# A four-layer graph kernel: two of the gated layer's turns issued together, a new order for the last groups of the message layer, and a new place for VectorE's first gated slots

## What is computed

```
x = layernorm(x + attention(x))        # exp(8 tanh(QK/8)) * adj, row sums, A @ x @ v
x = layernorm(x + gated(x))            # 5 steps: m = adj h; r, z = sigmoid(..); hv = tanh(..); h = (1-z) h + z hv
x = layernorm(x + chebyshev_conv(x))   # adj^k x for k = 0..3
x = layernorm(x + message(x))          # f = relu(x psi + b); m = (adj*adj) f; relu([m, x] phi1 + b) phi2 + b
```

## Time and profile before

| | us |
|---|---|
| median of 3 runs | 1379.63 |
| lowest and highest | 1378.92 and 1381.86 |
| the profiled execution | 1379.54 |
| its span, first to last instruction | 1377.8 |
| PE busy in it | 1337.2 (97%) |
| DVE busy | 1081.9 (79%) |
| ACT busy | 950.3 (69%) |
| POOL busy | 861.8 (63%) |

### The profile page before, as it was taken

One profiled execution on the slowest core, in us unless ns is written; L12 is line 12 of the kernel. 1 busy time (PEld: TensorE's weight loads), 2 busy tenths in 40 slices (PEclk: granted clock), 3 DMA queues, 4 the chain that ended last, 5 costly groups with the idle time before them and its releaser, 6 DMA issues.

```text
span 1377.8 us, 27560 instructions
## 1 busy us (share of the span) xinstructions
PE 1337.2 (97%) x8630; PEld 1186.4 (86%) x8630; DVE 1081.9 (79%) x2537; ACT 950.3 (69%) x1730; POOL 861.8 (63%) x907
## 2 busy tenths in 40 slices
PE   8999979999999999999999999999899999999995
PEld 6999967888888888888888888887689999999994
DVE  4788857777778777787777787777788888888885
ACT  4888857776777777777776777766546666666664
POOL 5988866666666666666666666665435555555554
PEclk9999999999999999999999999999999999999998
DMA  3233322000020000020000110000212222222211
GB/s 105 86 100 106 95 100 77 1 0 0 15 85 24 0 0 0 32 89 0 0 0 0 54 39 1 0 0 10 76 54 70 70 69 69 69 69 69 69 39 39
DMA packets 60048, 61.25 MB, mean 44 GB/s; under 512 B 4690, under 2 KB 39380, under 8 KB 59988
## 3 DMA queue, kind: packets, MB, share of 16 engines
q1 hardware_dynamic: 59556, 60.31, 13.9%
q10 hardware_dynamic: 432, 0.20, 0.1%
HBM read 35.33 MB, written 25.17 MB: 44 GB/s over the span
## 4 chain that ended last, share of the span: by engine, by line
PE 91%; DVE 4%; ACT 2%; POOL 2%; issue 1%; DMA 0%; ACTq 0%; POOLq 0%; DVEq 0%
PE psum L1039 6%; PE psum L733 5%; PE psum L735 5%; PE psum L721 5%; PE psum L382 4%; PE psum L1051 3%; PE psum L1053 3%; PE psum L776 3%; PE psum L765 3%; PE psum L748 3%; PE psum L777 3%; PE psum L746 3%; PE psum L778 3%; PE psum L766 3%; PE psum L768 3%; PE psum L769 3%
## 5 line engine op out<-in xcount | busy, mean ns | idle before, releaser
L696 POOL TENSOR_TENSOR rh_lo<-rh,rh_hi 128x512 fp32r<-128x512 f32 x160 | 207.0, 1294 | 264.3 <-ACT rh_hi L811 264.3
L702 POOL TENSOR_TENSOR h_lo<-h,h_hi 128x512 fp32r<-128x512 f32 x160 | 216.6, 1354 | 12.8
L811 ACT CAST rh_hi<-rh 128x512 fp32r<-128x512 f32 x160 | 99.4, 621 | 147.8 <-DVE rh L843 147.8
L824 DVE TENSOR_TENSOR psum<-psum,h 128x512 f32<-128x512 f32 x160 | 111.9, 699 | 102.4 <-ACT psum L815 102.4
L733 PE MATMUL psum<-adj_t_hi,hn_hi 128*128 128x256 f32 x640 | 172.6, 303 | 1.0 <-DVE m_lo L837 1.0
L808 ACT ACTIVATE psum<-psum,bias_cols 128x512 f32<-128x512 f32 x160 | 106.7, 667 | 79.2 <-PE psum L753 79.0
L735 PE MATMUL psum<-adj_t_hi,hn_lo 128*128 128x256 f32 x640 | 159.2, 283 | 0.0
L843 DVE TENSOR_TENSOR rh<-psum,h 128x512 f32<-128x512 f32 x160 | 110.1, 688 | 50.8 <-ACT psum L808 50.7
L733 PEld LDWEIGHTS psum<-adj_t_hi,hn_hi 128*128 128x128 f32 x640 | 122.2, 191 | 2.0 <-issue 2.0
L735 PEld LDWEIGHTS psum<-adj_t_hi,hn_lo 128*128 128x128 f32 x640 | 122.5, 191 | 0.0
L798 ACT ACTIVATE z<-psum,bias_cols 128x512 f32<-128x512 f32 x160 | 111.2, 695 | 0.0
(11 more groups left out here) (197 smaller groups left out, 4341.6 us busy)
## 6 DMA issues: line engine op xcount, KB each, us to landing
x_in<-in_x_dram SPq DMA_DIRECT2D x32, 256.0 KB, 3.0
x_dram<-x SPq DMA_DIRECT2D x32, 256.0 KB, 2.1
g_x<-x_dram SPq DMA_DIRECT2D x32, 256.0 KB, 3.1
h_dram<-h SPq DMA_DIRECT2D x32, 256.0 KB, 2.0
ht<-h_dram SPq DMA_DIRECT2D x32, 256.0 KB, 2.8
c_x<-x_dram SPq DMA_DIRECT2D x32, 256.0 KB, 3.1
out_dram<-res SPq DMA_DIRECT2D x32, 256.0 KB, 2.4
conv_in<-in_L_gnn_weight_dram SPq DMA_DIRECT2D x1, 448.0 KB, 4.8
```

What stands on the lines that cost most here:

```text
L696: pool.tensor_tensor(rh_lo[:, q, :], rh[:, q, :], rh_hi[:, q, :].bitcast(F32), ALU.subtract).then_inc(rh_lo_done, 1)
L702: pool.tensor_tensor(h_lo[:, q, :], h[:, (g - 1) % G, :], h_hi[:, q, :].bitcast(F32), ALU.subtract).then_inc(h_lo_done, 1)
L824: dve.tensor_tensor(cb, cb, hg, ALU.subtract).then_inc(dif_done, 1)
```

## The change

There are three parts.

1. **Turns in pairs.** In all gated slots except the first 8 and the last 8, PE turns the states of an even group and of the next, odd one together in the even slot, and turns nothing in the odd slot. The odd one goes to PSUM bank 7.
2. **A new end of the message layer.** Slots 34 to 37 go; each engine has a written list (`drain`) instead, in which groups 30 and 31 go side by side through the stages, in buffers and banks of the earlier stages that are free by then. The statistics of the last groups are made for 4 columns in place of 12. PE has 5 and later 3 products with no use of their result (`idle_products`). The last group's result is made one tile by ACT and three by DVE.
3. **VectorE's first gated slots.** The sums become a part of their own, and the first four gated slots stand between `slot` and the sums.

```diff
-    def run(eng, slot, lags, between=None, second=None):
+    def run(eng, slot, lags, between=None, second=None, third=None):
+        parts = [part for part in (slot, second, third) if part is not None]
...
         for s in range(GROUPS - U, GROUPS + lags):
+            for k, part in enumerate(parts):
+                part(s // U, s % U)
+                yield s if part is parts[-1] else s - 0.5 + k / 4
...
+        def sums(it, u):
+            s = it * U + u
             if live(it, u, LAG_OUT):
...
-        yield from run(dve, slot, LAG_NORM, weights, second=normalise)
+        yield from run(dve, slot, LAG_NORM, weights, second=sums, third=normalise)
...
+    def paired(base, g):
+        return not isinstance(base, int) or G <= base + g < SLOTS - G
...
+        def turn(base, g, k, bank):
+            s = base + g
...
+                pe.wait_ge(h_done, s - G + 1)
+            wait_count(pe, hn_lo_done, s - 1 if paired(base, g) and g > 0 else s)
...
+            if not paired(base, g):
+                if live(base, g, 0):
+                    turn(base, g, k, B_HN)
+            elif g % 2 == 0:
+                turn(base, g, k, B_HN)
+                turn(base, g + 1, k, B_HN_ODD)
...
+        def drain():                                   # POOL
+            pool.wait_ge(hid_mm, LAST - 1)
+            x3_with_bias(LAST - 1)
...
+            pool.tensor_tensor(rstd[:, 0, ln1], var_eps[:, 0, ln1], minus_half[:, ln1], ALU.pow).then_inc(rstd_x3_done, 1)
+            pool.wait_ge(x3_done, GROUPS)
+            halves_of_x3(x3t[:, :], x3t_hi[:, :], x3t_lo[:, :], LAST - 1)
+            halves_of_x3(end_x3t, end_x3t_hi, end_x3t_lo, LAST)
+            last_power(LAST - 2, ENTRY + 2)
+            x3_with_bias(LAST)
+            last_power(LAST - 1, ENTRY + 3)
+            last_power(LAST, ENTRY + 4)
...
+        def drain():                                   # PE
+            pe.wait_ge(hid_done, LAST - 1)
+            features(B_F, x3t, LAST - 1)
+            idle_products(5)
+            pe.wait_ge(x3_done, GROUPS)
...
+                mm = pe.transpose(psum[:, B_T1, cols(i)], x3[:, LAST % 4, i, :], ident[:, :])
...
+            messages(NEXT_MSG, f_hi, f_lo, LAST - 1)
+            features(END_F, end_x3t, LAST)
+            hidden_of_x3(B_F, x3t_hi[:, :], x3t_lo[:, :], LAST - 1)
+            hidden_of_message(B_F, msg_hi[:, :], msg_lo[:, :], LAST - 1)
...
+            messages(END_MSG, end_f_hi, end_f_lo, LAST)
...
+            outputs(B_M, hid, LAST - 1)
...
+            hidden_of_x3(END_HID, end_x3t_hi, end_x3t_lo, LAST)
+            hidden_of_message(END_HID, end_msg_hi, end_msg_lo, LAST)
+            idle_products(3)
+            outputs(END_O, end_hid, LAST)
...
+        def drain():                                   # ACT
...
+            turned(x3t[:, :], B_T23, LAST - 1)
+            result(LAST - 3, every)
...
+            features_hi(f_hi[:, :, :], B_F, LAST - 1)
...
+            turned(end_x3t, B_T1, LAST)
+            message_hi(msg_hi[:, :], NEXT_MSG, LAST - 1)
...
+            features_hi(end_f_hi, END_F, LAST)
...
+            hidden(hid[:, :], B_F, LAST - 1)
+            message_hi(end_msg_hi, END_MSG, LAST)
+            result(LAST - 2, every)
+            hidden(end_hid, END_HID, LAST)
+            result(LAST - 1, every)
+            result(LAST, every[:1])
```

More of the change, by code:

```diff
@@ L207, in attention_layer @@
     B_QKT, B_QK, B_ADJ, B_U, B_W = 4, 5, 6, 7, 2
-    def run(eng, slot, lags, between=None, second=None):
+    def run(eng, slot, lags, between=None, second=None, third=None):
+        parts = [part for part in (slot, second, third) if part is not None]
         for s in range(PEELED * U):
-            slot(s // U, s % U)
-            if second is not None:
-                second(s // U, s % U)
+            for part in parts:
+                part(s // U, s % U)
             if between is not None:
@@ L218, in run @@
             for u in range(U):
-                slot(it, u)
-                if second is not None:
-                    second(it, u)
+                for part in parts:
+                    part(it, u)
         for s in range(GROUPS - U, GROUPS + lags):
-            slot(s // U, s % U)
-            if second is not None:
-                yield s - 0.5
-                second(s // U, s % U)
-            yield s
+            for k, part in enumerate(parts):
+                part(s // U, s % U)
+                yield s if part is parts[-1] else s - 0.5 + k / 4
     def live(it, u, lag):
@@ L948, in run @@
                     second(it, u)
-        for u in range(lags):
-            slot(GROUPS // U + u // U, u % U)
+        for u in range(L_W):
+            slot(GROUPS // U, u)
     def live(it, u, lag):
@@ L998, in slot @@
                 sp.dma_start(out_view[:, bass.ds(n * TILES, TILES), :], res[:, u % 2, :, :]).then_inc(res_out[u % 2], 16)
-        yield from run(sp, slot, L_RES)
+        yield from run(sp, slot)
+        for n in range(GROUPS - 4, GROUPS):
+            sp.wait_ge(res_done, n + 1)
+            if n == LAST:
+                sp.wait_ge(res_half_done, 1)
+            sp.dma_start(out_view[:, n * TILES:(n + 1) * TILES, :], res[:, n % 2, :, :]).then_inc(res_out[n % 2], 16)
         for i in range(2):
@@ L1086, in slot @@
                 wait_count(pe, y1_done, s)
+                if isinstance(it, int) and s == 0:
+                    pe.wait_ge(earlier["hn_lo_done"], earlier["pairs_end"])
                 if isinstance(it, int) and s == 2:
@@ L1156, in slot, with features @@
                 mm.then_inc(x3t_mm, 1)
-        yield from run(pe, slot, L_F)
+        def features(bank, src, n):
+            pe.wait_ge(x3t_done, n + 1)
+            pe.matmul(psum[:, bank, :], ones[:, :], flat(psi_row[:, :, :]), start=True, stop=False, skip_group_check=True)
+            for i in range(TILES):
+                mm = pe.matmul(psum[:, bank, cols(i)], src[:, cols(i)], psi[:, :], start=False, stop=True,
+                               skip_group_check=True)
+            mm.then_inc(f_mm, 1)
@@ new lines, in messages @@
+        def messages(bank, hi, lo, n):
+            pe.wait_ge(f_lo_done, n + 1)
+            for b in range(GB):
+                dst = psum[:, bank, :].rearrange("p (c b n) -> p c b n", c=KC, b=GB)[:, :, b, :]
+                for k in range(KC):
+                    pe.matmul(dst, hi[:, tile(b, k), :], adj_sq[:, k, :], start=(b == 0 and k == 0), stop=False,
+                              skip_group_check=True)
+                    mm = pe.matmul(dst, lo[:, tile(b, k), :], adj_sq[:, k, :], start=False, stop=(k == KC - 1),
+                                   skip_group_check=True)
+            mm.then_inc(msg_mm, 1)
@@ L1159, in scalar @@
+        yield from run(pe, slot)
+        drain()
     def scalar(act):
@@ L1307, in slot, with combine @@
                 moments_of(LN1, lambda i: y2[:, i, :])
-        yield from run(dve, slot, L_Y3)
+        def combine(columns, p, count):
+            dve.tensor_tensor(moments[:, p, columns, :], stats[:, columns, 0:3], stats[:, columns, 3:6], ALU.add)
+            dve.tensor_tensor(parts[:, 0, columns], stats[:, columns, 1], stats[:, columns, 4], ALU.subtract)\
+               .then_inc(parts_done, 1)
+            dve.wait_ge(parts_done, count)
+            dve.tensor_scalar(parts[:, 1, columns], moments[:, p, columns, 2], 1.0 / D, EPS, ALU.mult, ALU.add)
+            dve.scalar_tensor_tensor(out=parts[:, 2, columns], in0=parts[:, 0, columns], scalar=0.25,
+                                     in1=parts[:, 0, columns], op0=ALU.mult, op1=ALU.mult)
+            dve.tensor_scalar(negmean[:, p, columns], moments[:, p, columns, 1], -0.5, None, ALU.mult)\
+               .then_inc(terms_done, 1)
+            dve.wait_ge(terms_done, count)
+            dve.tensor_tensor(var_eps[:, p, columns], parts[:, 1, columns], parts[:, 2, columns], ALU.add)\
+               .then_inc(var_done, 1)
@@ L1310, in graph_conv_layers @@
+        yield from run(dve, slot)
+        drain()
     return {"sync": sync, "gpsimd": gpsimd, "tensor": tensor, "scalar": scalar, "vector": vector}
```

172 lines of the change are left out of this document (150 added, 22 removed).

## The result

The changed kernel takes **1362.45 us** (median of 4 runs, 1361.78 to 1362.98) against 1380.12 (4 runs): a ratio of 0.9874, 95% interval 0.9859 to 0.9888. That is 17.7 us less. The prediction was 1367.3 with a range from 1363.0, so the gain was larger than foreseen and the time lies 0.55 us outside the range. The profiled execution took 1361.78 us with a span of 1360.0.

The account below looks back on a forecast made before the run. PE, busy 97% of the span at 2.4 GHz nearly throughout, was taken as the bound, with its waits at joints. 7.2 (handover) + 0.3 (pairs) + 4.75 (end) = 12.2 us off 1379.54 gave 1367.3 us, range 1363.0 to 1371.5.

Parts of the forecast that it names:

- The pairs: Steady gated layer: turning two groups' states together was to save 0.3 us in all, from 0 to 1.4.
- the switch: PE's change of kind between exact turns and reduced products, put at 0.00 to 0.02 us a pair.
- the pairs pay: Rival, 10%: PE saves 0.05 to 0.1 us a pair at changes of kind, giving 1360 to 1364 us.
- two slots differ from 9.7 by over 0.05: Sign that the prediction is wrong: two steady gated slots together differing from 9.7 us by more than 0.05.
- The handover, 7.2 forecast: Joint of attention and gated layer: moving VectorE's sums behind the first four gated slots was to gain 7.2 us.
- `hn_lo` of group 0 comes forward by the sums ahead of it: Handover's first step: `hn_lo` was to come 2.16 us sooner, letting PE turn group 1 earlier.
- POOL is not in the way: Handover: POOL's mask for PE's last weighted sum, done at 188.56 us, precedes that sum's new start at 191.76.
- The second half of the chain: Handover, VectorE from group 31's sums to `rh` of group 1: laid out as 2.16, 1.11 and 1.20 us.
- the upper bound of 8.3: Handover: the gain if PE followed its own list with no wait on VectorE, estimated at 8.3 us.
- The clock at the handover: Rival, 17%: the clock falls at the handover, or a ring there keeps part of the gain, giving 1368.2 to 1370 us.
- The end: Message layer's last groups: an earlier x3 and a shorter path to the last result were to gain 4.75 us.
- The interleaving: The end: group 30's work between group 31's turn and outputs was to delay group 31 by 1.0 us.

Follow-up runs that it names:

- handover_only: The kernel before with VectorE's order alone changed, the sums standing behind the first four gated slots: 1375.65 us, ratio 0.9973 to before.
- hn_lo_from_psum: The changed kernel, but `hn_lo` of groups 0 to 2 reads PSUM's bank 0 in place of x1 (wrong values, same work): 1358.87 us, ratio 0.9854 to before.
- pairs_only: The kernel before with the pairs of turns alone: 1373.95 us, ratio 0.9956 to before.
- after_again: The changed kernel, nothing altered, measured once more: 1362.29 us, ratio 0.9875 to before.
- stand-ins: Four kernels, each the changed kernel with unused TensorE work added behind its last products, run once each: 226 to 228 ns per 512-column product once settled.
- x1_through_psum: The changed kernel, with ScalarE copying x1 into PSUM's bank 0 in gated slots 0 to 2 for `hn_lo` to read: 1361.04 us, ratio 0.9862 to before.

## Why the prediction failed, point by point

- **The pairs, 0.3 us forecast, 6.7 measured.** This is the step that broke the range: "Nothing is left over for a switch: 0.00 to 0.02 us a pair by the rounding, 0 to 1.4 us in all. I take 0.3." The reading of the switch was right, and the table shows it: eight turns and the late product behind them cost 876 ns in both kernels. What I took for fixed was the price of all other products. 30 large ones at 3.1 ns less are 0.093 us a pair and the small ones give 0.027, together 0.12. 56 pairs between the two marks stand in the steady state: 6.7 us. The three times 8 slots in which a set loads a new x1 took 0.27 us more each (39.71 to 39.99), 0.8 in all, and from group 144 on the third stretch is 0.8 shorter, 0.44 of it by the turn that stands in the second stretch now. So the term that the forecast put at nothing without a reason is the start-to-start distance of the other products: rows 8 show it for the order of before only. Why the pitch changed stays open. The rival "the pairs pay" had 10%; its price (0.05 to 0.1 a pair) was somewhat low, and its reason, something saved at each change of kind, is not what the rows show. That its 1360 to 1364 us hold the measured time is luck, as it left the handover at 7.2. The same holds for how near the forecast came: the handover's shortfall hides part of the pairs' gain. That two slots differ from 9.7 by over 0.05 was named as what would prove the forecast wrong, and they do.
- **The handover, 7.2 forecast, 4.7 from the order** (handover_only; 4.4 in the changed kernel, whose second stretch holds a turn more). "`hn_lo` of group 0 comes forward by the sums ahead of it" is the step that failed. It started 2.1 us sooner and ended no sooner, since it has both operands in SBUF and met POOL's mask. So r of group 0 did not move (192.65 + 1.33 = 193.98, before 193.92, forecast 190.24), and neither did the last sums (196.16 + 1.33 = 197.49, before 197.43). I had written "POOL is not in the way" after looking only at the data that PE needs from it. The second half of the chain held: from `den` of group 31 to `rh` of group 1 I laid out 2.16 + 1.11 + 1.20 = 4.47, and it took 200.53 - 196.16 = 4.37, before 8.16. The 3.8 us gained there are all that the order gave in this chain. PE's third wait and the clock fall at 199.9 us are gone with it. With the mask out of the way (hn_lo_from_psum) the first two stretches are 191.72 + 47.84 - 184.44 - 45.52 = 9.6 us shorter than before, of which 1.6 stand ahead of the mask (179.83 to 178.21): 8.0, near the upper bound of 8.3 that I had given. No clock fall met the handover in that profile.
- **The clock at the handover** did fall, 187.8 to 191.2 us, as in the rival; it fell there before as well (189.6 to 193.0), so it cost the change nothing new.
- **The end, 4.75 forecast, 5.35 measured.** Right in mechanism, each term a little small. x3 follows the statistics by 1341.60 - 1338.77 = 2.83 us and not 3.08. Most of that is the first step: the moments, now of 4 columns, begin 0.90 us after the statistics do (1339.67 for 1338.77), where it was 1.08 in the rows that the forecast used (1371.09 for 1370.01). No run shows whether the 4 columns are the reason. From there to the turn 1.17, forecast 1.15. The interleaving cost 8.80 - 7.96 = 0.84, not 1.0. The last result came 1.30 sooner, not 1.07. The end's clock is not the reason: pairs_only and handover_only, with the old end, have one fall more there and 0.9 to 1.0 us more than before, and the comparison above is with the shorter one.
- **The first 1.2 us** belong to no part of the change. The kernel before had a clock fall at 19 us in its profile, the changed one had none. after_again, the same program as after, has none either and reaches r of group 0 only at 191.64 us, as PE waited there for the load of the input:

```profile
56.20 0.66 PE L366 MATMUL psum<-ident,x_in 128*128 128x128 f32 x4 [1.57 <-DMA x_in<-in_x_dram]
```

Measured parts by stretch, 1.21 + 4.41 + 6.70 + 0.13 + 5.35, give the 17.8 us of span.

## What to carry to other kernels

Before moving a VectorE instruction whose operands both lie in SBUF, look at what GpSimd does at the new time, not only at who delivers its data. The start-to-start distance of a product in a saturated TensorE stream is a number to measure again after each change of the order: 1.3% of it (232.0 to 228.9 ns in the mean) was worth more here than either of the other two parts. And expect 1 to 2 us of scatter in one profile from clock falls, and from a wait for a load, that come or do not come.

## What the runs showed of the hardware

- **VectorE beside GpSimd.** `hn_lo` from two SBUF operands took 2.84 and 2.51 us beside a GpSimd instruction of 2.4 us and ended 0.55 behind it; from PSUM and SBUF it took 0.66 beside the same one. The Trainium skill ("SBUF — State Buffer", Who interferes with whom) says that a VectorE instruction with two SBUF inputs contends with a GpSimd instruction that reads SBUF, and that whichever of two contending ones comes second is blocked in full. The trace agrees: `hn_lo` started 0.09 and 0.38 us after the mask and ended about as long after the mask's end as it takes alone (0.55 against 0.66). The prediction left this out.
- **TensorE's pitch has several steady values at a granted clock of 1.00.** For 512 columns of the reduced kind 226.7, 228.9 and 233.3 ns; for 256 columns 120.0 alone and 113 to 123 in the layer. The Trainium skill ("TensorE: Matmul & The Clock Gate", Back-to-back issue gap) gives 518 cycles for 512 columns, 216 ns at 2.4 GHz, for the gap of an isolated product; no run here shows that. What picks the value, and why every order in the real layer shows at least 228.9 while the stand-ins show 226.7, stays open. Shown is only that the bank of the turns, the counts in the loops and, in stand-ins, the operands, the other engines' accesses and satisfied waits do not bring the 233.3, and that one product more or a turn elsewhere leaves it.
- **Clock falls come and go between executions.** The order up to 175 us is the same in all 19 profiles; 8 of them show the clock at half for 3.4 us near 19 us. From POOL's first mask to its second they take 7.4 us, the other 11 take 5.8. (Between before and after 1.33 of these 1.6 us are left, as the first mask of before stood 0.28 earlier.) Windows from 18 to 22 us (us, PE busy, granted clock, DMA share, GB/s), the kernel before, with the fall:

```profile
18.00:22.00 4.00, 3.84 (x21) 0.62 0.02 4
```

and the changed one, without it, with the fall at the handover that both have:

```profile
18.00:22.00 4.00, 3.56 (x28) 1.00 0.01 4
188.00:191.00 3.00, 3.00 (x14) 0.50 0.00 0
```

  x1_through_psum, with the changed kernel's early order, has it too (0.60 there). At the joint of the gated layer and the convolution the fourth stretch is 366.9 to 367.1 us without a fall, 367.4 to 368.4 with one, 369.1 to 369.9 with two; after and after_again, the same program, had one and two.
- **A load comes late in some executions.** In 7 of the 19 profiles, with the same order up to there, PE waits 0.7 to 1.6 us for the load of the input near 56 us; in the other 12 it does not.
